# Retention scores and state products on 64 rows, one array half for each head parity

## The reference

```python
q = _rope(q, cos, sin) * dk ** (-0.5)          # 4 heads, dk = 64, dv = 128
k = _rope(k, cos, sin)
def step(S, inp):                              # one chunk of tokens
    qn, kn, vn = inp
    attn = einsum('bhid,bhjd->bhij', qn, kn) * Dmask
    o = einsum('bhij,bhjv->bhiv', attn, vn) + einsum('bhid,bhdv->bhiv', qn * cross, S)
    S = S * gC + einsum('bhid,bhiv->bhdv', kn * kdec, vn)
    return (S, o)
o = o * rsqrt((o ** 2).mean(-1) + EPS) * g_norm_w * (g * sigmoid(g))
out = o.reshape(B, T, 2 * D) @ Wo
```

## Time and profile before

| | |
|---|---|
| Median of 3 runs | 2890.27 us (2883.27 to 2890.65) |
| Profiled execution | 2889.12 us, span 2887.3 us |
| Mean granted TensorE clock | 0.977 |
| TensorE busy | 2761.1 us, 96% |
| VectorE busy | 2122.3 us, 74% |
| ScalarE busy | 1775.2 us, 61% |
| GpSimd busy | 1265.1 us, 44% |

### The profile page before, as it was taken

The page is one execution under the profiler, slowest core; times in us unless marked ns, Lnnn a source line. Parts: engine busy times, 40 slices in busy tenths (PEclk is TensorE's granted clock), DMA queues, the critical chain, the costliest instruction groups (busy, mean ns, idle before and its releaser), DMA issues.

```text
span 2887.3 us, 53204 instructions
## 1 busy us (share of the span) xinstructions
PE 2761.1 (96%) x19426; PEld 1531.9 (53%) x19426; DVE 2122.3 (74%) x4452; ACT 1775.2 (61%) x3798; POOL 1265.1 (44%) x1764
## 2 busy tenths in 40 slices
PE   4989999999999999999999999999999999999997
PEld 3843367533774338643486434854358533675334
DVE  5669946898468975689656895669956699467983
ACT  3428864488544885448754587536864378643884
POOL 2325544355442554335543455434553345433453
PEclk8979999999999999999999999999999999999999
DMA  6032000511016000150002400033000330004200
GB/s 188 29 89 45 2 30 30 126 22 38 8 33 143 16 23 8 47 130 16 31 1 61 115 16 31 1 88 88 17 30 26 93 60 16 30 30 106 42 2 15
DMA packets 71396, 139.16 MB, mean 48 GB/s; under 512 B 12752, under 2 KB 49664, under 8 KB 69984
## 3 DMA queue, kind: packets, MB, share of 16 engines
q1 hardware_dynamic: 71008, 135.72, 18.7%
q10 hardware_dynamic: 128, 0.03, 0.0%
HBM read 86.02 MB, written 38.82 MB: 43 GB/s over the span
## 4 chain that ended last, share of the span: by engine, by line
PE 71%; DVE 13%; issue 5%; POOL 5%; SPq 2%; DMA 2%; ACT 1%; POOLq 0%; DVEq 0%; ACTq 0%
PE psum L841 20%; PE psum L897 16%; DVE mx L1644 6%; PE psum L626 5%; PE psum L960 3%; PE psum L872 3%; PE psum L807 3%; PE psum L630 2%; PE psum L668 2%; PE psum L690 2%; PE psum L1042 2%; PE psum L1045 2%; DVE nrm L1492 2%; PE psum L1018 2%; POOL X L1759 1%
## 5 line engine op out<-in xcount | busy, mean ns | idle before, releaser
L1644 DVE TENSOR_REDUCE mx<-psum 128x1 f32<-128x512 f32 x2048 | 1266.0, 684 | 88.3 <-PE psum L841 87.6
L1353 ACT ACTIVATE Z<-psum 128x512 f32<-128x512 f32 x2048 | 1109.2, 598 | 281.3 <-PE psum L872 252.9
L1849 POOL TENSOR_TENSOR Z<-Z,W_low 128x256 f32<-128x256 f32 (+1 forms) x1152 | 713.2, 642 | 688.1 <-ACT Z L1353 681.0
L841 PE MATMUL psum<-SK,SQ 63*128 63x512 f32 x2048 | 800.4, 470 | 29.2 <-DVE mx L1644 22.9
L872 PE MATMUL psum<-SQ,SK 64*128 64x512 f32 x2048 | 758.4, 472 | 9.5 <-DMA SQ<-mrow 9.0
L897 PE MATMUL psum<-Z,Vx 128*17 128x256 f32 x8192 | 641.3, 387 | 0.4 <-POOL Z L1849 0.4
L841 PEld LDWEIGHTS psum<-SK,SQ 63*128 63x128 f32 x2048 | 329.6, 191 | 480.7 <-DVE mx L1644 360.0
L872 PEld LDWEIGHTS psum<-SQ,SK 64*128 64x128 f32 x2048 | 311.4, 189 | 81.3 <-ACT Z L1353 37.1
L897 PEld LDWEIGHTS psum<-Z,Vx 128*17 128x17 f32 x8192 | 138.2, 95 | 334.5 <-issue 275.7
L1794 POOL TENSOR_TENSOR Z<-Z 128x512 f32<-128x512 f32 x64 | 83.8, 1309 | 314.4 <-DVE Z L1547 314.4
L1759 POOL TENSOR_TENSOR X<-X,mixed 128x512 f32<-128x512 f32 x64 | 80.4, 1268 | 235.8 <-DVE mixed L1513 235.8
(11 more groups left out here) (137 smaller groups left out, 3759.8 us busy)
## 6 DMA issues: line engine op xcount, KB each, us to landing
W_low<-bias_rows SPq DMA_DIRECT2D x8, 2048.0 KB, 8.7
parts<-Z SPq DMA_DIRECT2D x32, 512.0 KB
W_low<-low_parts SPq DMA_DIRECT2D x7, 1536.0 KB, 6.6
X<-L_attn_a_x SPq DMA_DIRECT2D x8, 1024.0 KB, 5.5
SQ<-parts SPq DMA_DIRECT2D x32, 256.0 KB, 7.7
SK<-parts SPq DMA_DIRECT2D x32, 256.0 KB, 10.6
SQ<-parts SPq DMA_DIRECT2D x16, 512.0 KB, 6.6
SK<-parts SPq DMA_DIRECT2D x16, 512.0 KB, 14.1
```

What stands on the lines that cost most here:

```text
L841: pe.matmul(row_bank(c), SQ[rows_of(h, MAX_ROW), h // 2, i * P:i * P + P], SK[rows_of(h, MAX_ROW), h // 2, 512 * k:512 * k + 512], start=T ...
L1353: nc.scalar.activation(ring[:, n % RING, :], col_bank(n), ACT.Exp)\
L1644: nc.vector.tensor_reduce(mx2[:, blk % 2, col, k:k + 1], row_bank(2 * u + k), AX_X, ALU.max)\
L1849: nc.gpsimd.tensor_tensor(ring[:, n % RING, a:z], ring[:, n % RING, a:z], band_exp[:, 4 * hg + cols_of(s)[i], at:at + z - a], ALU.mult)\
```

## The change

A head's scores and its product with the state become matmuls of their own on the 64 partitions where the head's transposed queries and keys lie. The zeroed form `qbd` goes, with its clearing at the start; one copy brings all four blocks to `qkT`. Even heads write to bank 4, odd heads to bank 5: scores in columns 0 to 255, outputs (`o_of`) in columns 256 to 511. The state products now stand right behind the scores, and the masked scores are added onto them later. As scores and outputs share banks, the scores of a tile wait for `y_h` of the tile before (and for the state update). In t = 3 to 7 the scores, and `z_transposes`, move behind the value projection on TensorE, and `rope` moves ahead of the mask on VectorE. The mask reads from both banks.

```diff
-        qbd = sb("qbd", [P, 2, 2, 2, P])
+        qkT = sb("qkT", [P, 2, 4, P])
...
-        kq_T = tally("act", "kq_T", 3 * NT)
+        kq_T = tally("act", "kq_T", NT)
...
+        def o_of(h):
+
+            return bank[4 + h % 2][:, 256 + h // 2 * DV:256 + h // 2 * DV + DV]
...
-                if q == 0 and pr == 0:
-                    need(pe, att_m, b, NT)
-                if q == 0 and pr == 1:
+                if q == 0:
                     need(pe, y_h, b, 4 * NT)
...
+            def scores(b, u):
+
+                need(pe, kq_T, b, u + 1)
+                need(pe, att_m, b, u)
+                need(pe, s_upd, b, 2 * u)
+                need(pe, y_h, b, 4 * u)
+                if u == 0:
+                    need(pe, z_T, b, 8)
+                    need(pe, w_T, b - 1, 1)
+                for pr in range(2):
+                    for side in range(2):
+                        r = slice(DK * side, DK * side + DK)
+                        mm = pe.matmul(bank[4 + side][:, P * pr:P * pr + P], qkT[r, u % 2, 2 + pr, :],
+                                       qkT[r, u % 2, pr, :], start=pr == 0, stop=False, skip_group_check=True)
+                if u > 0:
+                    for pr in range(2):
+                        for side in range(2):
+                            r = slice(DK * side, DK * side + DK)
+                            mm = pe.matmul(o_of(2 * pr + side), qkT[r, u % 2, pr, :], S[r, pr, :],
+                                           start=False, stop=False, skip_group_check=True)
+                mm.then_inc(att.sem, 1)
...
-                    if 1 <= t <= NT:
-                        u = t - 1
-                        need(pe, kq_T, b, 3 * u + 3)
-                        need(pe, att_m, b, u)
-                        if u == 0:
-                            need(pe, z_T, b, 8)
-                        for pr in range(2):
-                            mm = pe.matmul(bank[4][:, 256 * pr:256 * pr + 256], kT[:, u % 2, pr, :],
-                                           qbd[:, u % 2, pr, :, :].rearrange("p a n -> p (a n)"),
-                                           start=True, stop=True)
-                        mm.then_inc(att.sem, 1)
-                    if t + 1 < NT:
+                    u = t - 1
+                    if t < 3:
+                        scores(b, u)
                         z_transposes(b, t + 1)
-                    if 0 < t < NT:
+                    if t < NT:
                         need(pe, v_cp, b, t)
                         if t == 1:
                             need(pe, x_att, b - 1, 3)
                         project(b, t, 1, 512, p_v)
-                    if 3 <= t <= NT:
+                    if t >= 3:
+                        scores(b, u)
+                        if t + 1 < NT:
+                            z_transposes(b, t + 1)
                         y_project(b, t - 3)
                     if t == NT:
                         y_transposes(b, NT - 2)
                     if 1 <= t <= NT:
                         need(pe, att_m, b, u + 1)
                         need(pe, v_cp, b, u + 1)
-                        need(pe, s_upd, b, 2 * u)
-                        need(pe, y_h, b, 4 * u)
-                        if u == 0:
-                            need(pe, w_T, b - 1, 1)
                         for h in range(RET_HEADS):
-                            o = bank[5][:, h * DV:h * DV + DV]
-                            mm = pe.matmul(o, AT[:, h * P:h * P + P], v_sb[:, u % 2, h * DV:h * DV + DV],
-                                           start=True, stop=u == 0)
-                            if u > 0:
-                                mm = pe.matmul(o, qbd[:, u % 2, h // 2, h % 2, :], S[:, h // 2, :],
-                                               start=False, stop=True)
+                            mm = pe.matmul(o_of(h), AT[:, h * P:h * P + P], v_sb[:, u % 2, h * DV:h * DV + DV],
+                                           start=False, stop=h >= 2, skip_group_check=True)
                         mm.then_inc(p_o.sem, 1)
...
-                        quad = bank[3].rearrange("p (a n) -> p a n", a=4)
-                        nc.scalar.copy(qbd[0:64, t % 2, :, 0, :], quad[0:64, 0:2, :]).then_inc(kq_T.sem, 1)
-                        nc.scalar.copy(qbd[64:128, t % 2, :, 1, :], quad[64:128, 0:2, :]).then_inc(kq_T.sem, 1)
-                        nc.scalar.copy(kT[:, t % 2, :, :], quad[:, 2:4, :]).then_inc(kq_T.sem, 1)
+                        nc.scalar.copy(qkT[:, t % 2, :, :], bank[3].rearrange("p (a n) -> p a n", a=4)).then_inc(kq_T.sem, 1)
...
+                    if 3 <= t < NT:
+                        rope(b, t)
                     if 1 <= t:
                         u = t - 1
                         need(dve, att, b, u + 1)
                         need(dve, p_o, b, u)
-                        nc.vector.tensor_tensor(AT[:, :], bank[4], mask[:, :], ALU.mult)\
+                        nc.vector.tensor_tensor(by_side(AT), psum[:, 4:6, 0:256].rearrange("p a (c n) -> p a c n", c=2),
+                                                by_side(mask), ALU.mult)\
                             .then_inc(att_m.sem, 1)
-                    if 0 < t < NT:
+                    if 0 < t < 3:
                         rope(b, t)
```

More of the change, by code:

```diff
@@ L170, in build @@
         qkr = cut(0, 1024).rearrange("p (a n) -> p a n", a=2)
-        kT = cut(1024, 512).rearrange("p (a c n) -> p a c n", a=2, c=2)
         AT = cut(1536, 512)
@@ L600, in _ @@
             pe.wait_ge(s_bank6, 1)
-            pe.wait_ge(s_zero, 6)
+            pe.wait_ge(s_zero, 5)
             pe.wait_ge(s_rowq, HEADS)
@@ L983, in gate_project @@
                 project(b, t, 2, 1024, p_g)
+            def scores(b, u):
[18 more added lines that the diff above has]
+                mm.then_inc(att.sem, 1)
             def qk_transposes(b, t):
                 need(pe, rope_qk, b, t + 1)
-                need(pe, kq_T, b, 3 * t)
+                need(pe, kq_T, b, t)
                 if t == 0:
@@ L1064, in _ @@
                 need(pe, gate, b, NT)
-                need(pe, kq_T, b, 3 * NT)
+                need(pe, kq_T, b, NT)
                 mix_k(b, 0, 0)
@@ L1274, in _ @@
                         for h in range(RET_HEADS):
-                            nc.scalar.activation(sq_junk[:, h * DV:h * DV + DV], bank[5][:, h * DV:h * DV + DV], ACT.Square,
+                            nc.scalar.activation(sq_junk[:, h * DV:h * DV + DV], o_of(h), ACT.Square,
                                                  accum_out=oss[:, u % 2, h:h + 1]).then_inc(o_sq.sem, 1)
@@ L1381, in link, with by_side @@
                 dve.wait_ge(s_chain, chain)
+            def by_side(w):
+                return w[:, :].rearrange("p (c a n) -> p a c n", a=2, c=2)
             def z_norms(b, t):
@@ L1408, in ln1_scales @@
                     .then_inc(ln1_sc.sem, 1)
-            for dst, value in ((power[:, :], -0.5), (nT[:, :, 0:1], 0.0), (qbd[:, :, :, :, :], 0.0),
+            for dst, value in ((power[:, :], -0.5), (nT[:, :, 0:1], 0.0),
                                (Vx[:, :, :, HD:HD + 1], 1.0), (S[:, :, :], 0.0), (nrm[:, 0, :], 1.0)):
@@ L1441, in _ @@
             ln1_scales(0)
-            dve.wait_ge(s_zero, 6)
+            dve.wait_ge(s_zero, 5)
             dve.wait_ge(s_rowq, HEADS)
@@ L1600, in _ @@
                         for h in range(RET_HEADS):
-                            nc.vector.scalar_tensor_tensor(y[:, h * DV:h * DV + DV], bank[5][:, h * DV:h * DV + DV],
+                            nc.vector.scalar_tensor_tensor(y[:, h * DV:h * DV + DV], o_of(h),
                                                            ors[:, u % 2, h:h + 1], gt[:, u % 2, h * DV:h * DV + DV],
@@ L1733, in _ @@
             prime(pool, "pool")
-            pool.wait_ge(s_zero, 6)
+            pool.wait_ge(s_zero, 5)
             pool.wait_ge(s_exp, 1)
```

## The result

The changed kernel takes 2875.48 us (median of 6 runs, 2872.52 to 2878.94); the kernel before, over 6 runs, 2887.92. The ratio is 0.9959, with a 95% interval of 0.9949 to 0.9969: faster by 0.4%. Forecast were 2877 us and a range of 2864 to 2891. The profiled execution spans 2876.0 us against 2887.3, 11.3 less.

A forecast was written before the change was run, and what follows sets the result against it. TensorE was taken to bound the middle tiles, t = 3 to 6. 4 x (-0.50) + 0.3 + 0 = -1.7 us a sequence, times eight 13.6: 2875.5 profiled, 2877 as median; range 2864 to 2891.

The forecast's parts named there:

- The group: Scores and state products on TensorE, tiles 3 to 6 (the middle tiles): 1.25 us in place of 1.75, saving 0.50 each.
- 8 steps: The group's 16 records run as pairs on both row halves: 8 steps of 0.111 us, 0.89 us.
- changing over: Going in and out of half-array work costs TensorE 0.36 us a stretch; a rival had it free, 2865 us, chance 0.06.
- The rival of halves one by one: The two halves don't overlap: group costs 2.14 us, +3.7 us a sequence, about 2919 us; chance 0.11.
- The rule's nine steps: Strict program order would give the group nine steps, 0.11 us more a middle tile, about 2880 us; the forecast rejected it.
- The place of the waits: Middle tiles: scores moved behind `y_h` with 1.0 us to spare, mask covered with 0.7 us; without the move, 0.4 wait.
- Tile 2: Scores start 0.66 us late behind `y_h` of tile 0, delaying mask, rope and decay: +0.3 us.
- Tiles 7 and 8: Masked product 1.2 us late in tile 7, +0.3; later scores 0.85 late, then 0.9 saved: about 0 together.
- In tile 1 nothing changes: Tile 1 waits for GpSimd's decay and gains nothing from a shorter TensorE.
- is hidden: ScalarE's one 512-column copy replacing three smaller ones stands behind the transposes, with the scores moved later: no cost.
- The borders eat it: Rival: tiles 2, 7 and 8 each lose 0.5 us, leaving -0.5 a sequence, 2886 us; chance 0.25.
- The granted clock: Rival: new waits bring one half-clock stretch into each retention stage, 2911 us, chance 0.03; a clock below 1 there would be wrong.

The follow-up runs named there:

- Experiment 3: Changed kernel with all eight 64-row matmuls on partitions 0 to 63, odd heads computed from even heads' operands: 2919.2 us, ratio 1.0107 to the kernel before.
- experiment 4: Changed kernel with the state products taken out of the group and put right ahead of the masked products, two half-array stretches a tile: 2893.75 us, ratio 1.0014.
- experiment 5: Changed kernel with its 64-row matmuls issued by half (both even heads, then both odd heads) instead of alternating: 2878.31 us, ratio 0.9969.
- Experiment 1: Changed kernel without its moves: scores and z_transposes ahead of the value projection in every tile, rotation behind the mask: 2884.26 us, ratio 0.9983.
- Experiment 6: Changed kernel with the moves of scores, z_transposes and rotation starting from tile 2 instead of tile 3: 2870.51 us, ratio 0.9943.
- Experiment 7: Changed kernel with the next norm's statistics moved, in tile 7, behind the mask, and their reciprocal root behind the decay: 2869.7 us, ratio 0.9939.

## Why the prediction was right

**The bound.** TensorE was the bound in the middle tiles and still is: 9.60 of 9.60 us busy after.

**The group.** Forecast 8 steps and 0.36 us of changing over, 1.25 us in place of 1.75, so 0.50 saved in each of tiles 3 to 6. Measured: 0.47 in tile 3 and 0.53 in tiles 4 to 6. The steps are the 0.111 us of the forecast; the 0.03 is in changing over, which leaves 1.75 - 0.53 - 0.89 = 0.33 us for the one stretch in place of 0.36. Experiment 3 shows that the overlap is the whole gain of the middle tiles, and experiment 4 the price of one more stretch, 0.40. The rival of halves one by one was priced at 2919 us; experiment 3 put it in place and took 2919.2. That close a hit is partly luck: the sequence lost 4.0 us and not 3.7, as tile 7 loses 0.4 too, and the 1.5 us of the first sequence were not in the price.

**The rule weighed.** "TensorE: Matmul & The Clock Gate", Part 3, "The mechanism", of the Trainium skill has matmuls start and end in program order. By that rule experiment 5 would have lost five steps; it lost one. In this kernel a half takes up its own matmuls though the other half's stand ahead of them. The rule's nine steps do not show in the changed kernel either: its records start in eight pairs. "TensorEngine Tiling (Array Packing)", "Key Properties", of the Trainium skill says that a change of mode drains the engine; experiment 4 agrees, with 0.40 us for a change in and out.

**The place of the waits.** Forecast: `y_h` at +1.84 and the scores at +2.9; measured +1.84 (436.59 less 434.75) and +2.94. The mask was forecast to end at +4.9 to +5.0, needed at +5.75; it ended at +4.84 and was needed at +5.73. Experiment 1 shows what the place is worth: without the moves most of the 0.5 us goes to a wait of 0.35 and its consequences. The copies of `z_transposes` end at 440.77, 0.7 us ahead of L1061: met, and less tightly than feared.

**Tile 2.** Forecast +0.3, measured +0.40. The scores waited 0.59 (0.66 late by the forecast), and the chain to the transposes ran as written: mask late, rotation late, decay ending at 414.68, L1015 at 414.74 after 0.30 idle. Experiment 6 shows that this order is the cause, as moving it gives 0.40 back.

**Tiles 7 and 8.** Forecast +0.3 and -0.3, together about 0. Measured +0.19 and -0.01 by the distances above. The masked product was 0.98 late in its tile (460.03 less the tile's start at 453.91, against 460.82 less 455.68; forecast 1.2), and the scores of tile 8 waited 0.87 for `y_h`. What the sum over both missed is 0.2 us a sequence, in tile 8: the masked product did come earlier, and with it the squares, 0.27 us counted from the transposes of tile 7, but GpSimd then took 0.50 us for a step that took 0.20 before, and the last head outputs gained nothing (below). Experiment 7 shows the statistics ahead of the mask as what held tile 7.

**The first sequence.** "In tile 1 nothing changes", and the single copy "is hidden": not in the first sequence, where the copy is waited for and the clock stands at 1.00 in place of 0.50 for 3.4 us. The forecast put these 2.0 us at nothing.

**The sum.** -1.7 us a sequence was forecast, -1.5 measured. Eight times that is 13.6 and 11.9 us; with the 2.0 of the first sequence the tiles give 13.9, and the medians differ by 12.4, which is as near as six runs with a spread of 6 to 7 us tell. The mechanism was right. That the total came within 1.5 us is in part luck: the 0.2 us a sequence too many and the 2.0 us left out nearly cancel. "The borders eat it" was the right place to look, but the borders took 0.6 us a sequence and not 1.5. The granted clock stood at 1.00 in the window shown and at 0.977 over the span, as before.

## What to carry to other kernels

Matmuls that spend half of the array's rows on zeros are worth splitting only if the halves run side by side: read it from starts a few nanoseconds apart in the same trace, and charge each stretch on half arrays its way in and out (here 0.40 us), so put all half-array work of a tile into one stretch. When outputs come to share a bank with earlier work, a new wait for the reader of that bank appears; place the writer behind work that doesn't need the bank, and look at the irregular first and last tiles by themselves: they gave up 0.6 of 2.1 us a sequence here, and put in order gave 1.1 back. Look at the first sequence too: a median over all of them hid 2.0 us.

## What I had not expected of the hardware

- The two row halves do not follow one list. With the matmuls ordered by half (experiment 5) four records of one half ahead of the other's cost one step of 0.11 us for a tile, where strict order would cost five.
- 64 rows cost the same as 128 when alone: 0.111 us a step in experiment 3, which is the step of the products on 128 rows.
- VectorE and GpSimd hinder each other, and the one that starts second pays. VectorE's `z_lows`, which reads two tiles of SBUF, took 0.41 us in the middle tiles before. There it ended before the decay began; now it falls beside it, and takes 0.95:

```profile
440.65 1.04 POOL L1814 TENSOR_TENSOR Z<-Z,decay 128x512 f32<-128x512 f32 x1
...
441.02 0.95 DVE L1529 TENSOR_TENSOR zT_both<-Z,zT_both 128x256 fp32r<-128x256 f32 x1
```

Over the whole trace of the changed kernel, the 25 of these operations with no decay beside them take 0.42 us on average, as the 56 of before do. The 39 that start while a decay runs all end 0.28 us after that decay ends, however long that is (0.63 to 1.32 us in all), and the decay keeps its 1.04. That is most of why VectorE's share of a middle tile grew from 5.86 to 6.49 us, off the path. In the trace of experiment 4 the order is the other way in 31 cases: `z_lows` starts first and keeps its 0.42 us, and the decay takes 1.23 in place of 1.04:

```profile
439.47 0.42 DVE L1533 TENSOR_TENSOR zT_both<-Z,zT_both 128x256 fp32r<-128x256 f32 x1
439.55 1.23 POOL L1818 TENSOR_TENSOR Z<-Z,decay 128x512 f32<-128x512 f32 x1
```

In tile 8 of the changed kernel it was on the path: GpSimd's small step (128 x 4 elements, 0.20 us in the tiles up to 6 and in tile 8 before) took 0.50 beside VectorE's L1513, in all eight sequences, and ended 0.06 us after it:

```profile
470.45 1.40 DVE L1513 SCALAR_TENSOR_TENSOR xkT<-nT,vec,xkT 128x512 f32<-128x512 f32 x2
...
471.42 0.50 POOL L1822 TENSOR_SCALAR oarg<-oss 128x4 f32<-128x4 f32 x1 [7.46 <-ACT Z L1284]
```

"GPSIMD Engine Reference", "1. Specifications", of the Trainium skill names contention with VectorE instructions that have two SBUF inputs; both of these have. The pairs here agree. No experiment was made for this; the cases compared differ in what else runs beside them.
